# A three-layer graph network in one launch: the second norm moves to ScalarE, small columns to GpSimd, and VectorE's work is dealt out anew over the feed-forward slots

## The chip, the core and the metric

One core of a Trainium2 chip runs the whole program in one launch. The metric is the device time of that launch in microseconds (us). A core has TensorE (PE in the profile, its weight loads PEld), VectorE (DVE), ScalarE (ACT), GpSimd (POOL) and SyncE (SP, here only the queue of DMAs). Each engine takes its instructions in the order written and waits on semaphores for the others.

## The reference, cut to what matters

Input x is 8 graphs of 1024 nodes with 256 features. A first attention stage makes x; then come three layers, of which each does this:

```
si = x @ attn_w[l, :d];  sj = x @ attn_w[l, d:]
scores = si[:, :, None] + sj[:, None, :] + attn_b[l]
scores = where(scores >= 0, scores, 0.2 * scores);  scores = where(mask, scores, -inf)
attn = softmax(scores, axis=-1)
agg = einsum('bij,bjd->bid', attn, x)
h = layernorm(x + agg, g1[l], beta1[l])
ff = gelu(h @ W1[l] + b1[l]) @ W2[l] + b2[l]
x = layernorm(h + ff, g2[l], beta2[l])
```

At the very end the result is layernorm(x0 + x), x0 being what entered the three layers. Everything is in float32; to get that from TensorE each product is made of three (high by high, low by high, high by low part), so each operand is split into `_hi` (ScalarE) and `_lo` (VectorE).

## The kernel before

The change touches only `graph_layers`. The work is cut into K = 48 chunks of 512 nodes (3 layers of C = 16; two chunks make a graph). One **round** k works on three chunks at once: it aggregates chunk k (attention times x), runs the feed-forward of chunk k-1, and norms chunk k-2. Within a round TensorE first does `aggregate(k)` (8 source tiles j, 12 products each), then `up(k-1, 0)`, `up(k-1, 1)` and the residual, and then 8 **slots** f, in each `up(k-1, f+2)` and `down(k-1, f)`. Sixteen of the 48 rounds belong to each layer; rounds 2 to 33 norm a chunk whose projections the next layer needs, rounds 34 to 49 norm chunks of the last layer, which get the final norm instead.

What VectorE makes in round k, in its written order:

- `p_lo(k, 3..7)`: low parts of the probabilities, each 128x512. ScalarE's `exps(k, j)` go before them (two passes each), TensorE's `aggregate(k)` waits for them one by one. `p_lo(k, 0..2)` come at the end of round k-1.
- in between, `stats2(k-2)` and `centred(k-2)`: statistics of the second norm, and (Y - mean) * g2 from PSUM, 4 passes of 128x256.
- `row_top(r)`: the largest neighbour value of 128 rows (128x1024, one per row tile, four a round). Before: one ahead of `h_lo`, one at f = 3, one at f = 5, one at the end of the round.
- `h_lo(k-1)`, 2 passes, for which `up` waits; `scaled(k-2)`, 4 passes of xo * rstd + beta2; `projections(k-2)`, 8 passes (or `final_stats`).
- `norm1(k)`: reciprocal of the softmax sums, 4 passes u = A * rinv + x, 4 `bn_stats`, 4 `bn_aggr`.
- the slots: `g_lo(k-1, f)` (low part of the gelu, for which `down(k-1, f)` waits), `score(k+1, f)`, `add_mask(k+1, f-1)`; twice `x_lo`; once `shift1` (the norm's -mean * rstd); in even rounds after the first `g_lo` also `row_columns` (4 operations on 128x8) and `v_prepare` (4 more).

GpSimd only makes `deviation1` and `deviation2`: the variance plus eps, to the power -0.5, on 128x4. ScalarE's gelu of slot f needs `up(f)` and `g_lo(f-2)`. SP's queue loads the masks of `row_top` (three buffers), the transposed mask of chunk k+2 (its second half waits for the last `add_mask` of the round), and stores xo.

## Time and profile before

| | us |
|---|---|
| median of 3 runs | 2660.37 (2658.11 to 2666.33) |
| the profiled execution | 2659.89 |
| its span in the trace | 2657.7 |
| busy, of the span: PE, PEld, DVE, ACT, POOL | 2399.8 (90%), 2201.3 (83%), 2365.4 (89%), 1703.0 (64%), 517.7 (19%) |
| first and last start of `norm1` | 638.58 and 2589.78 |

Busy time is how long an engine had an instruction in work. Instructions of one engine overlap at their ends, so what one costs in a row of like ones is the distance of their starts (its pitch), a little less than its own duration. Where an instruction was kept waiting, the timeline shows in square brackets how long, and whose end released it. TensorE's clock is shown as a share of its full speed.

### The profile page before, as it was taken

The numbers are of one execution on the slowest core, as the hardware profiler recorded it, in microseconds if no ns is written. First come the engines' busy times: TensorE is split into PE (matmuls) and PEld (weight loads), VectorE is DVE, ScalarE is ACT, GpSimd is POOL, SyncE is SP. The second block draws the span as 40 slices with busy tenths as digits, with TensorE's granted clock in tenths as the row PEclk, the third lists the DMA queues.
The fourth block names the chain that finished last, engine by engine and source line by source line (L and its number), as shares of the span: only waits on it lengthen the run. The fifth ranks groups of instructions, "written<-read, shape, count | busy, mean of one in ns | idle before, by whom it ended". The sixth has DMA issues, their size and how long they took to land.

```text
span 2657.7 us, 45899 instructions
## 1 busy us (share of the span) xinstructions
PE 2399.8 (90%) x16548; PEld 2201.3 (83%) x16548; DVE 2365.4 (89%) x5742; ACT 1703.0 (64%) x2681; POOL 517.7 (19%) x500
## 2 busy tenths in 40 slices
PE   8999999963999999999889999999989999999996
PEld 6999999953888888888788888888878888888886
DVE  5888888878899999999889999999998999999985
ACT  3444444433676776777767776776776677677673
POOL 3555555530000001001010100100000110111111
PEclk9999999986999999999999999999999999999998
DMA  4444444444332322313232232332323234232211
GB/s 148 127 137 141 143 143 135 140 127 109 92 80 64 88 76 76 93 52 88 85 106 58 79 88 72 88 84 60 88 84 103 64 96 108 81 99 81 59 40 40
DMA packets 349875, 247.32 MB, mean 93 GB/s; under 512 B 214480, under 2 KB 308688, under 8 KB 349648
## 3 DMA queue, kind: packets, MB, share of 16 engines
q1 hardware_dynamic: 349648, 244.39, 32.1%
q8 instruction: 131, 2.15, 0.3%
q14 instruction: 96, 0.79, 0.1%
HBM read 143.68 MB, written 50.33 MB: 73 GB/s over the span
## 4 chain that ended last, share of the span: by engine, by line
PE 30%; DVE 23%; ACT 16%; issue 7%; DMA 2%; SPq 1%; ACTq 0%; POOLq 0%; DVEq 0%; POOL 0%
ACT t L964 6%; ACT pT_hi L963 5%; PE Y L1422 5%; PE G L45 4%; PE G L43 4%; PE G L44 4%; PE Y L1424 4%; PE Y L1423 4%; DVE prod L1177 3%; DVE u L1120 3%; DVE xo L1163 3%; DVE xo L1156 2%; ACT L963 2%; DVE spare L1072 2%; DVE st L1124 2%
## 5 line engine op out<-in xcount | busy, mean ns | idle before, releaser
L991 ACT ACTIVATE g<-G,b_less 128x512 f32<-128x512 f32 x384 | 264.0, 688 | 522.5 <-PE G L45 398.3
L1371 PE MATMUL A<-x_hi,pT_hi 128*128 128x258 f32 x1536 | 446.9, 291 | 114.8 <-DVE pT_lo L1108 114.8
L1422 PE MATMUL Y<-w_hi,g_hi 128*128 128x256 f32 x1536 | 441.1, 287 | 77.2 <-DVE g_lo L1206 77.2
L1372 PE MATMUL A<-x_hi,pT_lo 128*128 128x258 f32 x1536 | 437.8, 285 | 0.0
L1373 PE MATMUL A<-x_lo,pT_hi 128*128 128x256 f32 x1536 | 437.1, 285 | 0.0
L1424 PE MATMUL Y<-w_hi,g_lo 128*128 128x256 f32 x1536 | 429.8, 280 | 0.0
L1423 PE MATMUL Y<-w_lo,g_hi 128*128 128x256 f32 x1536 | 429.3, 279 | 0.0
L1371 PEld LDWEIGHTS A<-x_hi,pT_hi 128*128 128x128 f32 x1536 | 295.2, 192 | 125.3 <-issue 112.8
L1422 PEld LDWEIGHTS Y<-w_hi,g_hi 128*128 128x128 f32 x1536 | 289.4, 188 | 105.6 <-DVE g_lo L1206 97.3
L1206 DVE TENSOR_TENSOR g_lo<-g,g_hi 128x512 fp32r<-128x512 f32 x384 | 262.5, 684 | 67.3 <-ACT g_hi L994 65.3
L43 PE MATMUL G<-h_hi,w_hi 128*128 128x512 f32 x768 | 311.2, 405 | 5.7 <-DVE h_lo L1201 5.2
L45 PE MATMUL G<-h_lo,w_hi 128*128 128x512 f32 x768 | 306.7, 399 | 0.0
L44 PE MATMUL G<-h_hi,w_lo 128*128 128x512 f32 x768 | 305.8, 398 | 0.0
L1108 DVE TENSOR_TENSOR pT_lo<-t,pT_hi 128x512 fp32r<-128x512 f32 x384 | 254.7, 684 | 51.9 <-ACT t L964 51.1
L1423 PEld LDWEIGHTS Y<-w_lo,g_hi 128*128 128x128 f32 x1536 | 289.4, 188 | 8.2
L1372 PEld LDWEIGHTS A<-x_hi,pT_lo 128*128 128x128 f32 x1536 | 294.8, 192 | 0.0
L1373 PEld LDWEIGHTS A<-x_lo,pT_hi 128*128 128x128 f32 x1536 | 294.6, 192 | 0.0
L1424 PEld LDWEIGHTS Y<-w_hi,g_lo 128*128 128x128 f32 x1536 | 289.7, 189 | 0.0
L1096 DVE SCALAR_TENSOR_TENSOR t<-rrow,v 128x512 f32<-128x512 f32 x384 | 286.0, 745 | 2.6 <-ACT rrow L938 2.6
L917 POOL TENSOR_TENSOR ve<-mv,eps 128x4 f32<-128x4 f32 x64 | 30.0, 469 | 1320.8 <-DVE mv L1146 1178.9
L963 ACT ACTIVATE pT_hi<-t,v 128x512 fp32r<-128x512 f32 x384 | 272.9, 711 | 7.2 <-PE A L1373 6.7
L964 ACT ACTIVATE t<-t,v 128x512 f32<-128x512 f32 x384 | 272.1, 709 | 0.0
(176 smaller groups left out, 5857.0 us busy)
## 6 DMA issues: line engine op xcount, KB each, us to landing
mask<-mask SPq DMA_DIRECT2D x192, 256.0 KB, 3.3
a_adj_t<-in_adj SPq DMA_DIRECT2D x64, 512.0 KB, 4.0
x_rows<-rows SPq DMA_DIRECT2D x24, 1024.0 KB, 7.4
mask<-a_mask SPq DMA_DIRECT2D x64, 256.0 KB, 4.3
rows<-xo SPq DMA_DIRECT2D x32, 512.0 KB, 2.9
a_xs<-in_x SPq DMA_DIRECT2D x9, 1024.0 KB, 9.5
x_rows<-in_x SPq DMA_DIRECT2D x8, 1024.0 KB, 7.9
rows<-a_xo SPq DMA_DIRECT2D x64, 128.0 KB, 3.7
```

What stands on the lines that cost most here:

```text
L43: pe.matmul(out, left_hi, right_hi, start=start, stop=False)
L44: pe.matmul(out, left_lo, right_hi, start=False, stop=False)
L45: return pe.matmul(out, left_hi, right_lo, start=False, stop=stop)
L963: act.activation(L.pT[0][:, n % P_RING, :], L.t[:, j, :], ACT.Exp, bias=bias).then_inc(L.s_exp, 1)
L964: act.activation(L.t[:, j, :], L.t[:, j, :], ACT.Exp, bias=bias).then_inc(L.s_exp, 1)
L1096: dve.scalar_tensor_tensor(L.t[:, j, :], L.rrow[:, 0, k % 2, :], L.v8[:, k // 2 % VS, j:j + 1], L.rrow[:, 1, k % 2, :], ALU.add, ALU.max). ...
L1371: pe.matmul(L.A[:, t, 0:DE], hi, L.x_hi[:, par, j, :], start=(j == 0), stop=False)
L1372: pe.matmul(L.A[:, t, 0:DE], lo, L.x_hi[:, par, j, :], start=False, stop=False)
L1373: mm = pe.matmul(L.A[:, t, 0:D], hi, L.x_lo[:, par, j, :], start=False, stop=(j == NT - 1))
L1422: pe.matmul(L.Y[:, t, :], hi, L.w2[0][:, f, :], start=False, stop=False)
L1423: pe.matmul(L.Y[:, t, :], hi, L.w2[1][:, f, :], start=False, stop=False)
L1424: mm = pe.matmul(L.Y[:, t, :], lo, L.w2[0][:, f, :], start=False, stop=last and t % 2 == 1)
```

## The change

- `centred` on VectorE goes. ScalarE's new `n2(k-2)` writes (Y - mean) * rstd from PSUM into xo, four passes of 128x256, after `h(k-1, ...)`. `scaled` becomes two passes of 128x1024: times g2, then plus beta2. The wait for g2's load moves from `centred` to `scaled`.
- `row_columns` and `v_prepare` move from VectorE to GpSimd; there the columns are made in two halves of seven operations on 128x4, and -mean * rstd of both norms is made there too (two more operations each). `vrow`, `ub` and `top` become double.
- `norm1` is split: `sums` comes after `g_lo` of slot 0, `stats1` in slot 2. The eight passes of `projections` go two at a time into slots 1, 3, 5 and 7. In the last layer `final_sum` goes to slot 1, `final_stats` to 3, `final_norm` to 6.
- Three `row_top` stand ahead of the slots now (two ahead of `h_lo`, one behind), one in slot 5, none at the end.
- At the start, scoring begins after six row tops, and the seven of the next graph come after the low parts of chunk 0.

```diff
+    def rows_made(k):
+
+        return [n for n in ([2] if k == 0 else [(k + 5) // 2] if k % 2 == 1 else []) if n < NB]
...
-                    sp.wait_ge(L.s_scaled, TC * (m + 1))
+                    sp.wait_ge(L.s_scaled, 2 * (m + 1))
...
+            def row_columns(n, part):
+
+                done = COLS * n + COLS // NCH * part
+                cs = slice(TC * part, TC * (part + 1))
+                pool.wait_ge(L.s_top, NT * n + TC * (part + 1))
+                if part == 0:
+                    pool.wait_ge(L.s_vprep, 4 * (n + 1))
+                pool.tensor_tensor(L.z[:, cs], L.ub[:, n % 2, cs], L.top[:, n % 2, cs], ALU.add).then_inc(L.s_cols, 1)
+                pool.tensor_scalar(L.small[:, 1, cs], L.ub[:, n % 2, cs], SLOPE, None, ALU.mult).then_inc(L.s_cols, 1)
+                pool.wait_ge(L.s_cols, done + 2)
+                pool.tensor_scalar(L.small[:, 0, cs], L.z[:, cs], 0.0, 1.0 - SLOPE, ALU.is_ge, ALU.mult).then_inc(L.s_cols, 1)
+                pool.wait_ge(L.s_cols, done + 3)
+                pool.tensor_scalar(L.small[:, 0, cs], L.small[:, 0, cs], SLOPE, None, ALU.add).then_inc(L.s_cols, 1)
+                pool.wait_ge(L.s_cols, done + 4)
+                pool.tensor_tensor(L.m[:, cs], L.small[:, 0, cs], L.z[:, cs], ALU.mult).then_inc(L.s_cols, 1)
+                pool.wait_ge(L.s_cols, done + 5)
+                if n >= 1:
+                    pool.wait_ge(L.s_rrowT, NCH * n)
+                pool.tensor_tensor(L.rcol[:, 0, cs], L.ub[:, n % 2, cs], L.m[:, cs], ALU.subtract).then_inc(L.s_cols, 1)
+                pool.tensor_tensor(L.rcol[:, 1, cs], L.small[:, 1, cs], L.m[:, cs], ALU.subtract).then_inc(L.s_cols, 1)
...
+                if k >= 1:
+                    pool.wait_ge(L.s_n1, TC * k)
...
+                pool.wait_ge(L.s_rs, 4 * k + 1)
                 pool.tensor_tensor(L.rstd[:, :], L.ve[:, :], L.half[:, :], ALU.pow).then_inc(L.s_rs, 1)
...
+                pool.tensor_tensor(L.nm[:, :], L.mv[:, :, 0], L.minus[:, :], ALU.mult).then_inc(L.s_rs, 1)
+                pool.wait_ge(L.s_rs, 4 * k + 3)
+                pool.tensor_tensor(L.nmr[:, :], L.nm[:, :], L.rstd[:, :], ALU.mult).then_inc(L.s_rs, 1)
+
+            def deviation2(m):
+                if m >= 1:
+                    pool.wait_ge(L.s_n2, TC * m)
+                pool.wait_ge(L.s_mv2, TC * (m + 1))
+                pool.tensor_tensor(L.ve2[:, :], L.mv2[:, :, 1], L.eps[:, :], ALU.add).then_inc(L.s_rs2, 1)
+                pool.wait_ge(L.s_rs2, 4 * m + 1)
+                pool.tensor_tensor(L.rstd2[:, :], L.ve2[:, :], L.half[:, :], ALU.pow).then_inc(L.s_rs2, 1)
+                pool.tensor_tensor(L.nm2[:, :], L.mv2[:, :, 0], L.minus[:, :], ALU.mult).then_inc(L.s_rs2, 1)
+                pool.wait_ge(L.s_rs2, 4 * m + 3)
+                pool.tensor_tensor(L.nmr2[:, :], L.nm2[:, :], L.rstd2[:, :], ALU.mult).then_inc(L.s_rs2, 1)
...
+            v_prepare(0)
+            for part in range(NCH):
+                row_columns(0, part)
+            v_prepare(1)
             for k in range(K + 2):
                 if k >= 2:
-                    deviation2(L.s_mv2, TC * (k - 1), L.s_rs2, k - 2)
-                i = k - 2 - (K - C)
-                if i >= 0:
-                    deviation2(L.s_fin_mv, TC * (i + 1), L.s_fin_rs, i)
+                    deviation2(k - 2)
+                if k % 2 == 0 and (k + 2) // 2 < NB:
+                    for part in range(NCH):
+                        row_columns((k + 2) // 2, part)
+                for n in rows_made(k):
+                    v_prepare(n)
                 if k < K:
                     deviation1(k)
+                if k - 2 >= K - C:
+                    deviation3(k - 2 - (K - C))
...
-                if n >= 1:
-                    act.wait_ge(L.s_top, NT * n)
-                act.activation(L.vrow[:, :].rearrange("p (c i) -> p c i", c=2), L.A[:, 2:4, :], ACT.Copy).then_inc(L.s_vrow, 1)
+                if n >= 2:
+                    act.wait_ge(L.s_top, NT * (n - 1))
+                act.activation(L.vrow[:, n % 2, :].rearrange("p (c i) -> p c i", c=2), L.A[:, 2:4, :], ACT.Copy).then_inc(L.s_vrow, 1)
...
-                    act.wait_ge(L.s_nmr, k + 1)
+                    act.wait_ge(L.s_rs, 4 * (k + 1))
                 act.activation(L.u[:, t, :], L.u[:, t, :], ACT.Identity, bias=L.nmr[:, t:t + 1],
                                scale=L.rstd[:, t:t + 1]).then_inc(L.s_n1, 1)
+
+            def n2(m):
+                act.wait_ge(L.s_rs2, 4 * (m + 1))
+                if m >= 1:
+                    act.wait_ge(L.s_xst, 16 * m)
+                for t in range(TC):
+                    act.activation(L.xo[:, t, :], L.Y[:, t, :], ACT.Identity, bias=L.nmr2[:, t:t + 1],
+                                   scale=L.rstd2[:, t:t + 1]).then_inc(L.s_n2, 1)
...
+                if k >= 2:
+                    n2(k - 2)
...
+                    if f == 3:
+                        for n in rows_made(k):
+                            copy_v(n)
...
-            def norm1(k):
+            def sums(k):
...
+
+            def stats1(k):
+                n = TC * k
...
-            def shift1(k):
-
-                dve.wait_ge(L.s_rs, 2 * (k + 1))
-                if k >= 1:
-                    dve.wait_ge(L.s_n1, TC * k)
-                dve.scalar_tensor_tensor(L.nmr[:, :], L.mv[:, :, 0], -1.0, L.rstd[:, :], ALU.mult, ALU.mult).then_inc(L.s_nmr, 1)
 
...
-            def centred(m):
-
-                if m >= 1:
-                    dve.wait_ge(L.s_xst, 16 * m)
+            def scaled(m):
+                dve.wait_ge(L.s_n2, TC * (m + 1))
                 if new_layer(m):
                     dve.wait_ge(L.s_g2_in, 32 * (layer_of(m) + 1))
-                dve.wait_ge(L.s_mv2, TC * (m + 1))
-                for t in range(TC):
-                    dve.scalar_tensor_tensor(L.xo[:, t, :], L.Y[:, t, :], L.mv2[:, t, 0:1], L.g2[:, :], ALU.subtract,
-                                             ALU.mult).then_inc(L.s_n2, 1)
-
-            def scaled(m):
-                dve.wait_ge(L.s_rs2, 2 * (m + 1))
-                for t in range(TC):
-                    dve.wait_ge(L.s_n2, TC * m + t + 1)
-                    dve.scalar_tensor_tensor(L.xo[:, t, :], L.xo[:, t, :], L.rstd2[:, t:t + 1], L.be2[:, :], ALU.mult,
-                                             ALU.add).then_inc(L.s_scaled, 1)
-
-            def projections(m):
+                dve.tensor_tensor(L.xo[:, :, :], L.xo[:, :, :], L.g2[:, :].unsqueeze(1).to_broadcast([P, TC, D]),
+                                  ALU.mult).then_inc(L.s_scaled, 1)
+                dve.wait_ge(L.s_scaled, 2 * m + 1)
+                dve.tensor_tensor(L.xo[:, :, :], L.xo[:, :, :], L.be2[:, :].unsqueeze(1).to_broadcast([P, TC, D]),
+                                  ALU.add).then_inc(L.s_scaled, 1)
+
+            def projections(m, tiles):
 
                 slot = m % C
-                dve.wait_ge(L.s_scaled, TC * (m + 1))
-                if new_layer(m):
-                    dve.wait_ge(L.s_aw_in, 32 * (layer_of(m) + 1))
-                for t in range(TC):
+                if 0 in tiles:
+                    dve.wait_ge(L.s_scaled, 2 * (m + 1))
+                    if new_layer(m):
+                        dve.wait_ge(L.s_aw_in, 32 * (layer_of(m) + 1))
+                for t in tiles:
                     for i in range(2):
...
+            def final_sum(m):
...
+                dve.wait_ge(L.s_scaled, 2 * (m + 1))
+                dve.tensor_tensor(L.xo[:, :, :], L.xo[:, :, :], L.x1[:, :, :], ALU.add).then_inc(L.s_fin, 1)
+
...
-            v_prepare(0)
-            for r in range(NT):
+            for r in range(NT - 2):
                 row_top(r)
-            row_columns(0)
-            v_prepare(1)
             for j in range(NT):
                 score(0, j)
                 add_mask(0, j)
+                if j == HALF - 1:
+                    for r in range(NT - 2, NT):
+                        row_top(r)
...
-            for r in range(NT, NT + NT - 1):
-                row_top(r)
...
                 tops = tops_of(k)
+                early = 3 if k >= 1 else 1
                 if agg:
                     p_lo(k, LEAD)
                 if old:
                     stats2(k - 2)
                 if agg:
-                    for j in range(LEAD + 1, NT - 1):
+                    for j in range(LEAD + 1, NT):
                         p_lo(k, j)
-                if old:
-                    centred(k - 2)
-                if agg:
-                    p_lo(k, NT - 1)
-                for r in tops[:1]:
+                if k == 0:
+                    for r in range(NT, NT + NT - 1):
+                        row_top(r)
+                for r in tops[:min(early, 2)]:
                     row_top(r)
                 if ffn:
                     h_lo(k - 1)
+                for r in tops[2:early]:
+                    row_top(r)
                 if old:
                     scaled(k - 2)
-                if projected:
-                    projections(k - 2)
-                elif old:
-                    final_stats(k - 2)
                 if ffn and new_layer(k - 1):
                     less_b2(layer_of(k - 1))
-                if agg:
-                    norm1(k)
                 for f in range(KF):
                     if ffn:
                         g_lo(k - 1, f)
-                    if f == 0 and k % 2 == 0:
-                        if (k + 2) // 2 < NB:
-                            row_columns((k + 2) // 2)
-                        if (k + 4) // 2 < NB:
-                            v_prepare((k + 4) // 2)
+                    if f == 0 and agg:
+                        sums(k)
+                    if f == 2 and agg:
+                        stats1(k)
+                    if f in (1, 3, 5, 7) and projected:
+                        projections(k - 2, (f // 2,))
                     if after:
                         score(k + 1, f)
                         if f >= 1:
                             add_mask(k + 1, f - 1)
-                    if f == 1 and old and not projected:
-                        final_norm(k - 2)
-                    if f == 2 and agg:
-                        shift1(k)
+                    if old and not projected:
+                        if f == 1:
+                            final_sum(k - 2)
+                        if f == 3:
+                            final_stats(k - 2)
+                        if f == 6:
+                            final_norm(k - 2)
                     if f in (4, 6) and k + 2 < K:
                         x_lo(k + 2, f // 2 - 2)
-                    if f in (3, 5):
-                        for r in tops[f // 2:f // 2 + 1]:
+                    if f == 5:
+                        for r in tops[early:]:
                             row_top(r)
                     if f >= 4 and agg and new_layer(k):
                         weights_lo(layer_of(k), f - 4)
@@ -1313,8 +1361,6 @@
                     add_mask(k + 1, KF - 1)
                 if agg and new_layer(k):
                     weights_lo(layer_of(k), KF - 4)
-                for r in tops[3:]:
-                    row_top(r)
                 if after:
                     for j in range(LEAD):
...
-                pe.wait_ge(L.s_cols, 4 * (k // 2 + 1))
+                pe.wait_ge(L.s_cols, COLS // NCH * (k + 1))
...
-                pe.wait_ge(L.s_vrow, min((k + 5) // 2, NB))
+                pe.wait_ge(L.s_vrow, 2 if k == 0 else min(k // 2 + 3, NB))
...
-                        if k % 2 == 0 and k + 4 < K:
-                            v_row((k + 4) // 2)
+                        for n in rows_made(k):
+                            v_row(n)
```

## Rows read from the trace of the kernel before

**Rows 1.** Windows: one round; busy us of each engine, PEclk, DMA share, GB/s.
```profile
1556.12:1597.13 41.01, 37.86 (x273) 35.04 (x272) 39.10 (x99) 30.06 (x47) 3.48 (x4) 1.00 0.24 65
```

**Rows 2.** Timeline, TensorE, one round: start, us, instruction, idle before and its releaser.
```profile
1581.97 0.36 PE L1371 MATMUL A<-x_hi,pT_hi 128*128 128x258 f32 x1 [1.55 <-DVE pT_lo L1108]
...
1594.42 0.39 PE L43 MATMUL G<-h_hi,w_hi 128*128 128x512 f32 x1
...
1601.23 0.38 PE L1422 MATMUL Y<-w_hi,g_hi 128*128 128x256 f32 x1 [1.57 <-DVE g_lo L1206]
```

**Rows 3.** Timeline, VectorE, the same round.
```profile
1581.14 1.29 DVE L1108 TENSOR_TENSOR pT_lo<-t,pT_hi 128x512 fp32r<-128x512 f32 x2
...
1594.36 0.42 DVE L1177 SCALAR_TENSOR_TENSOR prod<-xo,aw 128x256 f32<-128x256 f32 x1
...
1597.13 0.17 DVE L1113 RECIPROCAL rinv<-A 128x4 f32<-128x4 f32 x1
...
1598.92 1.40 DVE L1124 BATCH_NORM_STATS2 st<-u 128x6 f32<-128x256 f32 x4
...
1600.51 0.66 DVE L1206 TENSOR_TENSOR g_lo<-g,g_hi 128x512 fp32r<-128x512 f32 x1
...
1602.35 0.74 DVE L1096 SCALAR_TENSOR_TENSOR t<-rrow,v 128x512 f32<-128x512 f32 x1
...
1603.02 0.68 DVE L1102 TENSOR_TENSOR t<-t,maskT 128x512 f32<-128x512 f32 x1
...
1603.62 0.68 DVE L1206 TENSOR_TENSOR g_lo<-g,g_hi 128x512 fp32r<-128x512 f32 x1
...
1613.96 1.22 DVE L1072 CUSTOM_DVE_ANT_0 spare<-vrow,mask 128x1024 bf16<-128x1024 f32 x1
...
1615.11 0.68 DVE L1206 TENSOR_TENSOR g_lo<-g,g_hi 128x512 fp32r<-128x512 f32 x1
...
1621.34 1.29 DVE L1108 TENSOR_TENSOR pT_lo<-t,pT_hi 128x512 fp32r<-128x512 f32 x2
```

**Rows 4.** Timeline, ScalarE, the same round.
```profile
1588.01 0.71 ACT L964 ACTIVATE t<-t,v 128x512 f32<-128x512 f32 x1
...
1590.61 0.77 ACT L974 ACTIVATE h_hi<-G,shift,g 128x512 fp32r<-128x512 f32 x1
...
1596.60 0.68 ACT L994 ACTIVATE g_hi<-G,b_less 128x512 fp32r<-128x512 f32 x1
```

**Rows 5.** Timeline, VectorE: starts of the first operation of `norm1` in six rounds.
```profile
724.36 0.17 DVE L1113 RECIPROCAL rinv<-A 128x4 f32<-128x4 f32 x1
...
1292.88 0.18 DVE L1113 RECIPROCAL rinv<-A 128x4 f32<-128x4 f32 x1
...
1346.22 0.17 DVE L1113 RECIPROCAL rinv<-A 128x4 f32<-128x4 f32 x1
...
1434.70 0.18 DVE L1113 RECIPROCAL rinv<-A 128x4 f32<-128x4 f32 x1
...
2103.74 0.15 DVE L1113 RECIPROCAL rinv<-A 128x4 f32<-128x4 f32 x1
...
2470.01 0.15 DVE L1113 RECIPROCAL rinv<-A 128x4 f32<-128x4 f32 x1
```

**Rows 6.** Timeline, VectorE, a round of the last layer.
```profile
2263.85 1.23 DVE L1214 TENSOR_TENSOR xo<-xo,x 128x1024 f32<-128x1024 f32 x1
...
2273.17 1.38 DVE L1226 TENSOR_SCALAR xo<-xo,mv,rstd 128x256 f32<-128x256 f32 x4
```

**Rows 7.** Timeline, GpSimd: first an otherwise idle stretch, then the round above.
```profile
642.21 0.20 POOL L911 TENSOR_TENSOR ve<-mv,eps 128x4 f32<-128x4 f32 x1 [59.34 <-DVE mv L1129]
...
1600.67 0.55 POOL L911 TENSOR_TENSOR ve<-mv,eps 128x4 f32<-128x4 f32 x1 [12.47 <-DVE mv L1129]
...
1601.31 2.00 POOL L913 TENSOR_TENSOR rstd<-ve,half 128x4 f32<-128x4 f32 x1
```

**Rows 8.** Timeline, VectorE, two rounds after the first change of layer.
```profile
1381.97 1.66 DVE L1156 SCALAR_TENSOR_TENSOR xo<-Y,mv,g 128x256 f32<-128x256 f32 x4 [3.14 <-DMA be<-in_L_gnn_beta]
```

More of the change, by code:

```diff
@@ L672, in layer_buffers @@
     L.v2 = sb("v2", [P, VS, NT])
-    L.top = sb("top", [P, NT])
+    L.top = sb("top", [P, 2, NT])
     L.z = sb("z", [P, NT])
+    L.small = sb("small", [P, 2, NT])
     L.m = sb("m", [P, NT])
     L.rcol = sb("rcol", [P, 2, NT])
-    L.vrow = sb("vrow", [P, N])
+    L.vrow = sb("vrow", [P, 2, N])
     L.rrow = sb("rrow", [P, 2, 2, BANK])
@@ L775, in graph_layers @@
     HALF = NT // 2
+    COLS = 7 * NCH
     EARLY = 5
@@ L1005, in _ @@
             x_hi(0)
+            for part in range(2):
+                copy_rows(0, part)
             x_hi(1)
-            for k in range(2):
-                for part in range(2):
-                    copy_rows(k, part)
+            exps(0, 0)
+            for part in range(2):
+                copy_rows(1, part)
+            exps(0, 1)
             copy_v(1)
-            for j in range(LEAD):
-                exps(0, j)
-            for k in range(K + 1):
-                ffn = k >= 1
+            exps(0, 2)
+            for k in range(K + 2):
+                ffn = 1 <= k <= K
                 for j in range(LEAD, NT):
```

88 lines of the change are left out of this document (40 added, 48 removed).

## The prediction

> **What bounds the kernel now.** I read the windows first. In a full round TensorE is busy 37.86 of 41.01 us, VectorE 39.10, ScalarE 30.06, GpSimd 3.48, and TensorE's clock is granted in full [rows 1]. VectorE has the least air, but a busy share says nothing about which of its work is on the path. So next I looked at where TensorE stands still, in its own timeline. There are two gaps a round: 1.55 us ahead of `aggregate`, ended by `p_lo`, and 1.57 us ahead of `down(0)`, ended by `g_lo` [rows 2]. Everything else of TensorE is packed. Its own work thus needs 41.01 - 1.55 - 1.57 = 37.9 us, and both gaps are VectorE's doing.
>
> VectorE's and ScalarE's timelines show why [rows 3, 4]. I count from the start of `p_lo(k, 0)` at 1581.14. Aggregation starts at +0.83, `up(0)` at +13.28 [rows 2], and ScalarE's second gelu pass of slot 0 ends at 1597.28, so +16.14 [rows 4]. `g_lo(0)` could start there. It starts at 1600.51, +19.37: VectorE is first held by projections (1594.36 to 1597.13), sums (to 1598.92) and statistics (to 1600.51) [rows 3]. From `g_lo(0)` to the next `p_lo(0)` it then has 1621.34 - 1600.51 = 20.83 us of slots [rows 3]. So the round is one loop: `p_lo(0)`, all that VectorE does before `g_lo(0)`, the slots, `p_lo(0)`. Over 14 rounds of the first layer it takes (1292.88 - 724.36) / 14 = 40.61 us, even and odd together [rows 5].
>
> **What the change makes of that loop.** After it, the stretch before `g_lo(0)` holds less for VectorE and the slots hold more. Two questions decide: does VectorE still reach `g_lo(0)` last, and how long are the slots?
>
> *Up to `g_lo(0)`.* The last exponential ends at 1588.72, +7.58 [rows 4], so `p_lo(7)` ends by +8.2 (pitch of a 128x512 pass with two inputs: 1603.62 - 1603.02 = 0.60 [rows 3]). Two row tops at 1615.11 - 1613.96 = 1.15 each [rows 3] bring +10.5, `h_lo` (2 x 0.60) +11.7, which is ahead of `up(0)` at +13.28; the third top +12.9. `scaled` is now two wide passes. The trace has one such pass, the last layer's sum, at 1.23 us [rows 6]; with the wait of the second for the first I take 2.5. It needs `n2`. ScalarE is done with `h` at 1591.38, +10.24 [rows 4]. No row shows a 256-column pass from PSUM on it; the nearest is the 512-column `h` at 0.77 [rows 4]. Half of that is the lower bound, the whole the upper: 4 passes are 1.5 to 3.1 us. I take 2.2, since a pass has a fixed part. `n2` then ends at +12.4, at worst +13.3, and `scaled` at +15.4, at worst +15.8. ScalarE has no gelu to make until `up(0)` is through, so `n2` is hidden in its wait. All of this is before +16.14. So TensorE's aggregation and ScalarE's gelu now end last, and `g_lo(0)` starts at about +16.2. What is taken off VectorE here (`centred`, half the fixed cost of `scaled`) buys nothing beyond that point: the rest becomes VectorE's idle time, 0.4 to 0.8 us or more.
>
> *The slots.* By pitches [rows 3]: eight `g_lo` 4.80; eight scores at 1603.02 - 1602.35 = 0.67, 5.36; eight `add_mask` 4.80; two `x_lo` 1.20; sums 1598.92 - 1597.13 = 1.79; statistics 1600.51 - 1598.92 = 1.59; projections 1597.13 - 1594.36 = 2.77; one row top 1.15. Together 23.46 us, where 20.83 stood: 6.15 come in; two tops, `shift1` and some waits on ScalarE go out. The columns (`row_columns`, `v_prepare`) leave VectorE here too, in even rounds, so even and odd rounds become alike.
>
> The new loop is 16.2 + 23.4 = **39.6 us**, above TensorE's 37.9, so VectorE's slots and the aggregation share the path and TensorE's two gaps become one, ahead of `aggregate`, with a short one at `down(7)`. Gain 1.0 us a round. TensorE is not late anywhere else: `down(1)` to `down(6)` follow their `g_lo` by one to three us.
>
> *The last layer* differs. No projections (2.77) but 1.23 + 1.59 + 1.38 = 4.2 us of final sum, statistics and norm [rows 3, 6], and these now all fall in the slots: 16.2 + 23.4 - 2.8 + 4.2 = 41.0. Before, it was (2470.01 - 2103.74) / 9 = 40.70 [rows 5]. These rounds lose 0.3 each.
>
> *Changes of layer.* Between 1292.88 and 1346.22 one round takes 53.34 us because weights arrive two pieces at a time [rows 5]; that chain goes through VectorE's and ScalarE's slots in the same way and I leave it. The two rounds after it take 88.48 [rows 5], 44.2 each. In the second of them `centred` waits 3.14 us for beta2 to land [rows 8]; the wait now belongs to `scaled`, some 6 us later in the round, where the load is there or nearly. So I take 2 x 39.6 here: 9.3 gained, and 8 at the second change, where one of the two is already a last-layer round.
>
> *GpSimd.* It gets 14 small operations in an even round, 4 in an odd one, and two more for each norm. One takes 0.20 us in a quiet stretch and 0.55 in the round; the power takes up to 2.00 [rows 7]. Deviation 2, whose statistics stand between the low parts, is made before the row tops; 14 columns at 0.65 with their waits take 9 us from the first row top at +9.4, so until +18.5; TensorE reads them in slot 2, past +21. Deviation 1: the statistics end at +24.0, then 0.55 + 2.00 + 0.55 + 0.55 and gaps, ready at +28. `n1` stands behind gelu(5), which ends at about +29. All hidden; without that cover the columns would cost their 9 us. What waits behind `n1` on ScalarE is gelu(6), and VectorE asks for that only at about +34.
>
> *Loads.* SP issues the masks after the round's last `add_mask`. That moment now lies right at `p_lo(0)` and the first row top stands earlier, so their lead shrinks by some 2 us. The store waits for `scaled`, a little later than before, and `n2` of the next round for the store, most of a round later: nothing.
>
> *Head and tail.* At the head seven row tops (8 us) move behind the first low parts, and scores start after six tops and a GpSimd chain. At most 8 us, at least 0; I take 5 with the first two rounds, since these tops still stand before the first `sums`. At the tail nothing hides the chain: two more GpSimd operations, `n2` in place of `centred` that ran beside GpSimd, a wider `scaled`: +3.
>
> **Sum.** 27 rounds x 1.0 = -27; changes of layer -17; nine last-layer rounds +3; head -5; tail +3: -43. Against the profiled execution's 2659.9 (its span plus 2.2 around it, within 0.5 of the median 2660.4) that gives **2616 us**.
>
> **A rule against the change.** GpSimd's variance sum takes 0.55 in place of 0.20 us while VectorE is working, and VectorE's `g_lo` beside it starts its successors on the usual pitch [rows 3, 7]. So the trace has GpSimd paying and VectorE not. The Trainium skill says more (SBUF — State Buffer, section "Who interferes with whom"): a VectorE instruction with two SBUF inputs and a GpSimd instruction that reads SBUF exclude each other for a whole instruction, and who starts first decides. Nearly all of VectorE's slot work is of that kind. The trace agrees with the one half; the other half, VectorE held, no row here shows. As a mechanism of this kernel it is the third rival below.
>
> **The rivals.**
> 1. *The changes of layer keep their time* (weights, loads of g2, and TensorE's clock after long gaps): only the 27 rounds gain. -26 with the other terms, 2634. For it: I argued these 17 us from a wait of 3.14 and a loop, not from a walk through them.
> 2. *VectorE isn't held at +16.2 or the slots overlap better*, and TensorE's 37.9 is approached. At 38.5 a round: -30 more, 2585. Against it: the slots' pitches are measured, and no idle time is in them.
> 3. *Slower: GpSimd holds VectorE.* If each of the four operations of deviation 1 and the 18 of the columns and preparation stop a VectorE instruction for their free 0.20 (the power for about 1.0), slots and run-up lose 1.6 and some 2 us: the loop passes 41.6. From 1.0 us lost a round the gain is gone; at 2 it is +27 in the 27 rounds and +20 in the last layer, less the changes of layer: about 2685. Against it: the two operations per norm that are there today cost VectorE nothing visible.
> 4. *No change:* a new wait takes about 1 us a round (masks that land late ahead of the three row tops, `n1` held by GpSimd by over 4 us, or `scaled` held so that `g_lo(0)` is at +17.2): 2655.
>
> **Chances.** The forecast 0.60 (own range 2604 to 2628), rival 1 0.15, rival 2 0.05, rival 3 0.10, rival 4 0.10. A measurement here can tell about 0.3%, 8 us. Faster takes the forecast, rivals 1 and 2 and a little of 4: 0.82; same 0.07; slower 0.11. The range reaches from a loop of 39.2 with the head at its bound, 2600, to rival 1 with a loop 0.3 worse, 2643.
>
> **What would show it.** Starts of the reciprocal 39.6 us apart, equal in even and odd rounds, and 41.0 in the last layer; VectorE idle for a microsecond or so ahead of `g_lo(0)`, released by ScalarE's gelu; TensorE's gap ahead of `down(0)` gone and the one ahead of `aggregate` over 2 us; no wait on GpSimd in ScalarE's list. It is wrong if `g_lo(0)` still stands behind VectorE's own work, if VectorE's 128x512 passes show a pitch above 0.60 beside GpSimd's, or if row tops wait for masks.

## The result and the profile after

The changed kernel takes 2622.18 us (median of 4 runs, 2618.43 to 2623.29) against 2659.89 for the kernel before: a ratio of 0.9848, with 0.9833 to 0.9862 as its interval. The forecast was 2616, range 2600 to 2643. The profiled execution took 2618.43 us, its span 2616.6.

First the windows of two successive rounds of the kernel after, cut at the starts of the reciprocal (columns: length, busy time and count of each engine, granted clock, DMA share, GB/s):

```profile
1529.73:1569.26 39.53, 37.01 (x266) 34.35 (x265) 37.04 (x85) 30.96 (x50) 8.63 (x12) 1.00 0.31 75
1569.26:1608.77 39.51, 37.54 (x274) 35.02 (x273) 37.30 (x84) 31.89 (x51) 14.67 (x22) 1.00 0.30 86
```

Against [rows 1], VectorE's busy time has fallen by 2 us and GpSimd's has risen from 3.48 to 8.63 and 14.67. Both rounds last 39.5 us, as forecast (39.6).

VectorE's timeline of the same kernel, one run-up to `g_lo(0)`:

```profile
1552.53 2.49 DVE L1166 TENSOR_TENSOR pT_lo<-t,pT_hi 128x512 fp32r<-128x512 f32 x4
...
1558.69 0.69 DVE L1166 TENSOR_TENSOR pT_lo<-t,pT_hi 128x512 fp32r<-128x512 f32 x1 [0.28 <-ACT t L1041]
1559.31 1.22 DVE L1143 CUSTOM_DVE_ANT_0 spare<-vrow,mask 128x1024 bf16<-128x1024 f32 x1
...
1561.83 1.28 DVE L1248 TENSOR_TENSOR h_lo<-h,h_hi 128x512 fp32r<-128x512 f32 x2
...
1564.18 1.22 DVE L1206 TENSOR_TENSOR xo<-xo,g 128x1024 f32<-128x1024 f32 x1
1565.43 1.22 DVE L1209 TENSOR_TENSOR xo<-xo,be 128x1024 f32<-128x1024 f32 x1
1568.65 0.69 DVE L1253 TENSOR_TENSOR g_lo<-g,g_hi 128x512 fp32r<-128x512 f32 x1 [2.00 <-ACT g_hi L1079]
1569.26 0.17 DVE L1171 RECIPROCAL rinv<-A 128x4 f32<-128x4 f32 x1
```

and ScalarE's and TensorE's of that stretch:

```profile
1561.22 1.92 ACT L1065 ACTIVATE xo<-Y,nmr,rstd 128x256 f32<-128x256 f32 x4
...
1567.35 0.69 ACT L1076 ACTIVATE g<-G,b_less 128x512 f32<-128x512 f32 x1 [2.91 <-PE G L45]
1567.93 0.68 ACT L1079 ACTIVATE g_hi<-G,b_less 128x512 fp32r<-128x512 f32 x1
```

```profile
1553.36 0.36 PE L1417 MATMUL A<-x_hi,pT_hi 128*128 128x258 f32 x1 [1.60 <-DVE pT_lo L1166]
...
1565.76 0.40 PE L43 MATMUL G<-h_hi,w_hi 128*128 128x512 f32 x1
...
1570.78 0.28 PE L1468 MATMUL Y<-w_hi,g_hi 128*128 128x256 f32 x1
```

Counted from `p_lo(0)` at 1552.53, aggregation starts at +0.83, `up(0)` at +13.23, `n2` ends at +10.6, and the second wide pass of `scaled` ends at +14.1. VectorE then stands still for 2.00 us until ScalarE's gelu lets `g_lo(0)` go at +16.12. In every other round the last low parts wait 1.0 us for ScalarE's exponentials first, and 0.99 us is left ahead of `g_lo(0)`; the start is at +16.12 all the same:

```profile
1529.12 0.69 DVE L1253 TENSOR_TENSOR g_lo<-g,g_hi 128x512 fp32r<-128x512 f32 x1 [0.99 <-ACT g_hi L1079]
```

Before, there was no such wait and `g_lo(0)` stood at +19.37 [rows 3]. TensorE has no gap ahead of `down(0)` any more (1570.78 has no bracket); the one ahead of `aggregate` is 1.60, as before [rows 2].

GpSimd's timeline, and then its lines by group for 1569 to 2000 us (busy us, mean ns of one, idle before):

```profile
1576.69 2.08 POOL L966 TENSOR_TENSOR ve<-mv,eps 128x4 f32<-128x4 f32 x1 [14.08 <-DVE mv L1190]
1578.85 1.10 POOL L968 TENSOR_TENSOR rstd<-ve,half 128x4 f32<-128x4 f32 x1
```

```profile
L966 POOL TENSOR_TENSOR ve<-mv,eps 128x4 f32<-128x4 f32 x11 | 22.9, 2086 | 119.2 <-DVE mv L1190 119.2
...
L977 POOL TENSOR_TENSOR ve<-mv,eps 128x4 f32<-128x4 f32 x10 | 10.9, 1091 | 167.1 <-DVE mv L1200 167.1
...
L948 POOL TENSOR_TENSOR z<-ub,top 128x4 f32<-128x4 f32 x10 | 5.2, 522 | 0.0
...
L953 POOL TENSOR_SCALAR small<-small 128x4 f32<-128x4 f32 x10 | 10.0, 1004 | 0.8
```

Of its small operations one costs 0.2 to 2.1 us in this stretch, where [rows 7] had 0.20 and 0.55 for the variance sum. It is hidden all the same, as the chain of waits for 900 to 2600 us shows (us in total, times, longest):

```profile
DVE g_lo L1253 <- ACT g_hi L1079: 95.5, 56, 5.0
...
DVE xo L1206 <- ACT xo L1065: 7.8, 7, 2.3
ACT xo L1065 <- POOL nmr L982: 7.4, 9, 1.7
...
DVE spare L1143 <- DMA mask<-mask: 3.4, 6, 0.9
...
ACT u L1057 <- POOL nmr L971: 0.9, 1, 0.9
```

Where did the 41.1 us of span go? The starts of `g_lo(0)` in both timelines cut the span into stretches that mean the same in both kernels:

| stretch | before | after | difference | forecast |
|---|---|---|---|---|
| start to `g_lo(0)` of round 2 | 727.73 | 722.11 | -5.6 | -5 |
| rounds 2 to 16, 14 of them | 568.53 | 553.39 | -15.1 | -14 |
| three rounds at the first change of layer | 141.82 | 135.09 | -6.7 | -9.3 |
| 13 rounds of the second layer | 527.53 | 513.76 | -13.8 | -13 |
| three rounds at the second change | 141.48 | 137.80 | -3.7 | -8 |
| nine rounds of the last layer | 366.27 | 367.22 | +1.0 | +3 |
| last three rounds | 119.78 | 121.00 | +1.2 | 0 |
| from there to the end | 64.56 | 66.23 | +1.7 | +3 |

The first row can't be counted for the change. In a second trace of the same changed kernel this stretch took 727.36 us, and in the traces of the kernels below 721.70 to 728.37. Of the 5.6 us, 3.6 lie ahead of the first row top (587.66 before, 584.11 after). The full rounds, in contrast, agree within 0.2 us over 14 and over 13 of them in the changed kernel's two traces.

### The profile page after: what moved, and what is told of

Its sections match the earlier page's. It is cut to its first block, busy times and chain, and to the rows that moved or that the text cites. A ratio compares the mean times of both kernels' runs of the same rounds, so it can differ in the third digit from the quotient of the medians.

```text
span 2616.6 us, 46231 instructions
## 1 busy us (share of the span) xinstructions
PE 2385.6 (91%) x16548; PEld 2200.0 (84%) x16548; DVE 2293.9 (88%) x5214; ACT 1793.4 (69%) x2873; POOL 986.1 (38%) x1125
## 4 chain that ended last, share of the span: by engine, by line
DVE 24%; PE 18%; issue 6%; ACT 2%; DMA 0%; POOL 0%; POOLq 0%; SPq 0%; DVEq 0%; ACTq 0%
DVE t L1154 5%; PE A L1417 5%; DVE t L1160 5%; PE A L1418 4%; PE A L1419 4%; DVE g_lo L1253 4%; DVE prod L1224 2%; DVE x_lo L1232 1%; DVE st L1185 1%; DVE spare L1143 1%; DVE u L1178 1%; PE G L1399 1%; PE G L45 1%; ACT g_hi L1079 1%; PE G L43 1%
## 5 line engine op out<-in xcount | busy, mean ns | idle before, releaser
L977 POOL TENSOR_TENSOR ve<-mv,eps 128x4 f32<-128x4 f32 x48 | 53.6, 1117 | 711.7 <-DVE mv L1200 711.7
L966 POOL TENSOR_TENSOR ve<-mv,eps 128x4 f32<-128x4 f32 x48 | 91.2, 1901 | 528.9 <-DVE mv L1190 528.9
L1166 DVE TENSOR_TENSOR pT_lo<-t,pT_hi 128x512 fp32r<-128x512 f32 x384 | 247.4, 691 | 37.4 <-ACT t L1041 37.2
```

## Experiments

All kernels start from the changed one. Ratios are to the kernel before, measured on the same chip; it took 2658.9 to 2660.8 us there. The changed kernel, measured a second time (beside the kernels of 4, 8 and 9), took 2621.12, 0.9846 (0.9824 to 0.9868).

**1. The second norm back on VectorE.** `centred` comes back between `p_lo(6)` and `p_lo(7)`, `scaled` is four passes again, `n2` is gone:

```diff
-                if k >= 2:
-                    n2(k - 2)
...
+                if old:
+                    centred(k - 2)
+                if agg:
+                    p_lo(k, NT - 1)
```

> Edit: the second norm goes back to VectorE (four passes of Y - mean times g2 ahead of the last p_lo, then four narrow passes with rstd and beta2), all else as in the changed kernel. My theory (a round is one loop: from p_lo(0) over TensorE's aggregation and ScalarE's gelu to g_lo(0), then VectorE's slots): VectorE gets 1.57 us more and 0.9 us less ahead of g_lo(0), where it idles 1.6 to 2.0 us, so the loop stays at 39.5 us and the time within 5 us of the changed kernel's 2622; the tail gets some 3 us shorter, and at a change of layer the fold waits less. Rival (VectorE's busy time sets the round): 0.7 us more in each of 46 rounds, 2652.

Measured: 2627.13 us, 0.9878 (0.9862 to 0.9895). The 13 rounds of a layer are 39.5 us each, as with `n2`. So in the rounds the new norm is worth nothing; its work was in the wait ahead of `g_lo(0)`. In all it is worth 5 us by the medians, and by the ratios (0.9878 against 0.9848 and 0.9846) 8 us, hardly more than the intervals allow. The traces show gains and losses. The round after the weights round is 43.46 and 44.35 us without `n2`, where it was 39.54 and 39.53, and the waits name the reason, the one of [rows 8]:

```profile
DVE xo L1204 <- DMA be<-in_L_gnn_beta: 10.9, 2, 5.9
```

The weights rounds themselves are shorter without `n2` (54.52 and 55.14 us), and so is the tail (63.97 against 66.2).

**2. and 3. The columns back on VectorE, in two places.** `row_columns` and `v_prepare` as before the change, once behind `g_lo(0)`, once ahead of it, in the wait:

```diff
+                columns(k)
```

ahead of the loop over the slots, or in it:

```diff
                     if ffn:
                         g_lo(k - 1, f)
+                    if f == 0:
+                        columns(k)
```

> Edit: row_columns and v_prepare go back to VectorE, behind g_lo of slot 0 (one of them in each round, about 0.7 us of small operations), all else as in the changed kernel. My theory: they lengthen the slots one for one, loop 40.2 us, and with 46 rounds about +30 us: 2650. Rival (GpSimd's many small operations hold VectorE): taking them off GpSimd gives part of it back, loop 39.5 to 39.8, 2622 to 2635. A GpSimd operation will also be shorter.

> Edit: as the kernel with the columns on VectorE in slot 0, but placed behind scaled, ahead of g_lo(0), where VectorE idles 1.6 to 2.0 us. My theory: the same operations are free here, loop 39.5 us, time 2622 within 5 us. Rival (VectorE's busy time sets the round, or GpSimd holds it): the same time as the kernel with them in slot 0.

Measured: in the slot 2641.07 us, 0.9933 (0.9917 to 0.9949), rounds of 39.9 and 40.1; ahead of `g_lo(0)` 2619.13, 0.9845 (0.9827 to 0.9864), rounds of 39.52. The same operations cost some 20 us behind `g_lo(0)`, and nothing that can be told from the noise ahead of it, one pass of 0.6 us earlier. The slots grow by 0.35 us in one round (`v_prepare`) and 0.57 in the next (`row_columns`), 0.46 on average, and the round by as much: one for one, as the first expectation has it, which had taken the operations at 0.7 us and so came to 2650. A timeline of the second kernel shows why: with them VectorE still waits.

```profile
1571.17 0.22 DVE L1096 TENSOR_SCALAR ub<-uv,ab 128x8 f32<-128x8 f32 x1
...
1573.13 0.69 DVE L1242 TENSOR_TENSOR g_lo<-g,g_hi 128x512 fp32r<-128x512 f32 x1 [1.59 <-ACT g_hi L1027]
```

So moving the columns to GpSimd was not needed for this gain. Once the order leaves a wait ahead of `g_lo(0)`, they fit there.

**4. Twelve more operations on GpSimd a round**, on 128x4 data of their own:

```diff
+                    for i in range(12):
+                        if 12 * k + i:
+                            pool.wait_ge(L.s_extra, 12 * k + i)
+                        pool.tensor_tensor(L.extra[:, i, :], L.eps[:, :], L.minus[:, :], ALU.mult).then_inc(L.s_extra, 1)
                     deviation1(k)
```

> Edit: twelve more operations of 128x4 with two inputs on GpSimd in each round, ahead of the first norm's deviation; they compute nothing that is used. My theory: hidden, GpSimd has 25 us of idle time a round; loop 39.5 us, time as the changed kernel within 3 us, VectorE's pitches as they are (0.60 for 128x512). Rival 3 of the prediction (GpSimd's reads hold VectorE): each costs VectorE up to 0.20 us, 2.4 us a round, partly in its idle time: loop 40.5 or more, 2665.

Measured: 2622.39 us, 0.9856 (0.9833 to 0.9879); rounds of 39.53. A window of one round:

```profile
1537.58:1577.10 39.52, 36.99 (x267) 34.32 (x266) 37.07 (x84) 30.96 (x50) 20.20 (x32) 1.00 0.34 76
```

GpSimd is now busy half the round (before the change: 3.48 of 41 us), and VectorE's busy time is still 37.07. Its 128x512 passes with two inputs keep their pitch of 0.60, and its slots stay at 23.41 us. Rival 3, GpSimd stopping VectorE by enough to be seen in a round, is refuted.

**5. The order back, the rest kept.** Projections, sums and statistics ahead of `g_lo(0)` again, row tops in their old places:

```diff
-                early = 3 if k >= 1 else 1
+                early = 1
...
+                if projected:
+                    projections(k - 2, range(TC))
+                if agg:
+                    sums(k)
+                    stats1(k)
                 for f in range(KF):
```

> Edit: VectorE's old order (projections, sums and statistics ahead of g_lo(0); row tops in slots 3 and 5 and at the end; final norm's parts as before), with the second norm on ScalarE and the columns on GpSimd kept. My theory: g_lo(0) is again held by VectorE's own work, at about +19.2, and the slots are 19.5 us plus about 1 us of waits on ScalarE: loop 39.8 us, even and odd alike, time about 2635. So most of the gain would come from the columns leaving the slots and from what is shed ahead of g_lo(0), and 0.3 us a round from the dealing. Rival (the dealing is what gains): loop 40.4 or more, 2655.

Measured: 2751.66 us, 1.0358 (1.0324 to 1.0392). This expectation failed: 2635 was expected, 2655 by its rival, and the rounds alternate at 41.4 and 43.9. The new norm and the columns on GpSimd, without the dealing out, make the kernel 3.6% slower than it was. Its rows, VectorE, TensorE and windows:

```profile
1545.55 1.23 DVE L1206 TENSOR_TENSOR xo<-xo,g 128x1024 f32<-128x1024 f32 x1 [1.12 <-ACT xo L1065]
...
1554.23 0.67 DVE L1253 TENSOR_TENSOR g_lo<-g,g_hi 128x512 fp32r<-128x512 f32 x1
```

```profile
1554.94 0.39 PE L1467 MATMUL Y<-w_hi,g_hi 128*128 128x256 f32 x1 [3.08 <-DVE g_lo L1253]
...
1556.42 0.59 PE L43 MATMUL G<-h_hi,w_hi 128*128 128x512 f32 x1
1556.81 0.63 PE L44 MATMUL G<-h_hi,w_lo 128*128 128x512 f32 x1
```

```profile
1515.00:1519.00 4.00, 4.00 (x26) 3.56 (x25) 3.98 (x7) 2.05 (x3) 2.84 (x3) 1.00 0.00 0
...
1556.40:1560.40 4.00, 4.00 (x18) 3.34 (x16) 2.88 (x5) 2.02 (x3) 2.86 (x3) 0.57 0.01 2
```

Two things were not in my sum. `scaled`, which in the old order is reached early, waits 1.12 us for `n2`, so `g_lo(0)` stands at +20.76 instead of +19.37. And TensorE's gap ahead of `down(0)` has grown to 3.08 us; behind it, in every second round, 4 us pass at a granted clock of 0.57 (mostly the lower of its two levels, 1.2 GHz), and a product over 512 columns takes 0.63 us instead of 0.39. In the other rounds the gap is as long (3.10 at 1513.52) and the clock stays at 1.00. Two more kernels took these apart.

**6. The same, with `up(2)` computed twice** into the same bank. It gives TensorE six more products in that gap and changes no result:

```diff
-                for i in range(KD):
+                for i in [i for _ in range(2 if f == 2 else 1) for i in range(KD)]:
```

> The order of before with the new norm and the columns on GpSimd (as in the kernel that took 2751.7 us), and one addition: the up product of the third feed-forward slot, up(2), is computed twice into the same bank, so that TensorE has 1.4 us less of idle time ahead of down(0). In that kernel's trace the gap ahead of down(0) was 3.08 us in each round, and in every second round (43.9 us, against 41.4) the granted clock stood at 0.57 from 1.5 us behind the gap on, for 4 us, and matmuls of 128x512 took 0.63 us instead of 0.39. Theory A (the long gap lowers the granted clock, and that costs the 2.5 us): with the gap at 1.7 us, as long as the one that the kernel before has there, the clock stays at 1.00, all rounds are 41.4 us, and 20 rounds win 2.5: about 2700 us. Theory B (the rounds of 43.9 us are those in which vcol's rows are transposed, and that work costs the 2.5 us by itself): the distances stay 41.4 and 43.9, about 2752 us. Theory C (TensorE's own work is what sets the pace of this order): the six extra matmuls, 1.4 us, are added in 47 rounds, up to 2815 us.

Measured: 2720.73 us, 1.023 (1.0213 to 1.0247). The gap ahead of `down(0)` and a window at the place where the clock was down:

```profile
1537.87 0.39 PE L1467 MATMUL Y<-w_hi,g_hi 128*128 128x256 f32 x1 [1.66 <-DVE g_lo L1253]
```

```profile
1541.00:1545.00 4.00, 4.00 (x32) 3.70 (x31) 3.91 (x6) 2.55 (x4) 1.19 (x1) 1.00 0.01 2
```

More work on TensorE makes the kernel 31 us faster: the gap is 1.66, the clock stays full, the long rounds fall from 43.9 to 42.3. Theory A holds for 1.6 of the 2.5 us. The last 0.9 is left; it stands in the rounds in which the `vcol` rows are transposed and copied, where theory B has it.

**7. The order back and the norm back** (the edits of 1 and 5 together). Of the change the columns on GpSimd, the first norm's `nmr` there and the new start stay.

> The order of before and the norm of before (both norm passes on VectorE); of the change only the small columns on GpSimd stay, with their double buffers. Theory A (the order with the new norm lost by its 1.1 us wait of scaled for ScalarE's n2 and by the clock behind the long gap; the columns on GpSimd cost nothing in either order): g_lo(0) comes at +19.4 us behind p_lo(0) as in the kernel before, the gap ahead of down(0) is 1.6 us, the clock stays up, and the columns' 0.8 us is out of every second round: 40.2 us in all, 2660 - 0.8 x 23 = about 2642 us (2635 to 2650). Theory B (the columns or the first norm's small operations on GpSimd come late in the old order): rounds of 41 us or more, 2690 to 2750 us. In both the rounds at the two changes of layer keep the times of the kernel before, 53 and 44 us.

Measured: 2651.64 us, 0.9970 (0.9957 to 0.9983). VectorE's `g_lo(0)` and the next `p_lo(0)`, two rounds:

```profile
1636.59 0.66 DVE L1257 TENSOR_TENSOR g_lo<-g,g_hi 128x512 fp32r<-128x512 f32 x1
...
1657.26 1.29 DVE L1161 TENSOR_TENSOR pT_lo<-t,pT_hi 128x512 fp32r<-128x512 f32 x2
...
1676.64 0.66 DVE L1257 TENSOR_TENSOR g_lo<-g,g_hi 128x512 fp32r<-128x512 f32 x1
...
1698.16 1.28 DVE L1161 TENSOR_TENSOR pT_lo<-t,pT_hi 128x512 fp32r<-128x512 f32 x2
```

The slots are 20.67 and 21.52 us, before the change 20.83 [rows 3] and 21.64. The time lies above theory A's 2635 to 2650: with the columns gone from VectorE, even and odd rounds still differ, by 0.9 us (40.03 and 40.92). VectorE waits for the gelu twice in the long round, 1.66 us in all, where the short round has one wait of 0.88:

```profile
1685.33 0.69 DVE L1257 TENSOR_TENSOR g_lo<-g,g_hi 128x512 fp32r<-128x512 f32 x1 [0.53 <-ACT g_hi L1076]
...
1689.02 0.69 DVE L1257 TENSOR_TENSOR g_lo<-g,g_hi 128x512 fp32r<-128x512 f32 x1 [1.13 <-ACT g_hi L1076]
```

Before the change the long round had the columns (0.9 us by experiment 2) and waits of 0.66 and 0.13 us. So two branches of nearly the same length lie behind that difference, and taking the columns off VectorE alone uncovers the other: it wins 0.1 to 0.2 us a round.

Read as a path, the kernels give each part a price. Columns on GpSimd and the new start take 2660 to 2651.64 us; the dealing out, with the old norm, takes it to 2627.13 (experiment 1), some 24 us and the only large step; the norm on ScalarE takes it to 2622. Against experiment 5 the old norm is 100 us faster in the old order: 1.39 us in each of 46 rounds (`g_lo(0)` back from +20.76 to +19.37) and the 1.6 us of the clock in every second one make 101. In the new order it is 5 to 8 us slower.

**8. and 9. More work into the wait.** VectorE stands still ahead of `g_lo(0)` for 2.00 and 0.99 us in turn. If 1.6 to 2.0 us there are free, as I took it, a fourth row top (1.2 us), or that and one projection, should go there for nothing and make the slots shorter:

```diff
-                early = 3 if k >= 1 else 1
+                early = 4 if k >= 1 else 1
...
+                if projected:
+                    projections(k - 2, (0,))
```

(the last two lines in the second kernel alone, which leaves that projection out of slot 1)

> Edit: the fourth row top too stands ahead of the slots (behind h_lo) in place of slot 5. My theory: the slots lose 1.15 us, the stretch ahead of g_lo(0) has 1.6 to 2.0 us of air: loop 38.4 us, in the last layer 39.6, time about 2573. What could spoil it: its mask has only three buffers and is loaded only after the first row top of the round, so it may wait some tenths of a us. Rival (VectorE's busy time sets the round): no change, 2622.

> Edit: as the kernel with four row tops ahead of the slots, and the first pair of projections too ahead of g_lo(0), in place of slot 1. My theory: the slots lose 0.7 us more (in rounds that project), the air ahead of g_lo(0) is used up; TensorE's own work, 37.0 us in odd rounds and 37.9 in those with the extra transposes, and the chain from the last gelu over the first exponentials come close: loop 37.8 to 38.2 us in the first two layers, 39.6 in the last, time about 2560.

Measured: 2613.73 us, 0.9822 (0.9802 to 0.9842), rounds alternating at 38.38 and 39.80; 2615.72, 0.9833 (0.9812 to 0.9854), rounds of 38.8 and 39.5. Both expectations failed: of 49 us expected the first kernel gives 8, and the projections add nothing to it. A round of the first two layers gives 0.4 of the 1.15 us, and the last layer nothing (40.9 us on average, 39.6 expected): the row tops' masks, which the expectation named, are waited for there for 6.7 us in all, 2.6 at most (2050 to 2500 us). VectorE's timeline of the first kernel, in a long round:

```profile
1508.33 1.40 DVE L1166 TENSOR_TENSOR pT_lo<-t,pT_hi 128x512 fp32r<-128x512 f32 x2
1510.26 0.69 DVE L1166 TENSOR_TENSOR pT_lo<-t,pT_hi 128x512 fp32r<-128x512 f32 x1 [0.54 <-ACT t L1041]
1511.49 0.69 DVE L1166 TENSOR_TENSOR pT_lo<-t,pT_hi 128x512 fp32r<-128x512 f32 x1 [0.53 <-ACT t L1041]
...
1516.40 0.73 DVE L1166 TENSOR_TENSOR pT_lo<-t,pT_hi 128x512 fp32r<-128x512 f32 x1 [0.53 <-ACT t L1041]
...
1525.76 0.69 DVE L1253 TENSOR_TENSOR g_lo<-g,g_hi 128x512 fp32r<-128x512 f32 x1
```

The shorter slots bring VectorE to `p_lo(0..4)` before ScalarE's exponentials are done: three waits of 0.53 to 0.54 and one of 0.19. It then reaches `g_lo(0)` at +17.4 with its own work, without a wait, instead of at +16.1. VectorE's run-up had become the longer branch. It had least room in this parity before: the changed kernel has the 0.99 us wait there. ScalarE makes the exponentials without a gap behind the last gelu, and that one waits for TensorE's `up(7)`; shorter slots of VectorE don't bring it forward by as much.

**10. Two projections ahead instead.**

```diff
+                if projected:
+                    projections(k - 2, (0, 1))
...
-                    if f in (1, 3, 5, 7) and projected:
+                    if f in (5, 7) and projected:
```

> The changed kernel with two of the four projections of a round (1.4 us of VectorE's work) ahead of g_lo(0), where VectorE waits 2.0 us for the gelu, instead of in slots 1 and 3; the third row top stays where it is. Theory A (the loop is p_lo(0), aggregation, up(0), gelu, and then VectorE's slots alone): each round is 1.4 us shorter, 38.1, and the time 2622 - 1.4 x 31 = 2578 us. Theory B (what one more row top ahead showed: half of the rounds are then paced by ScalarE's exps, which the shorter slots reach before they are done, so that VectorE comes to g_lo(0) late): distances alternate at 38.4 and 39.5 or so, about 2600 to 2616 us. Theory C (the masks' transfers held the kernel with one more row top): no wait here for masks, and the time falls under 2590.

Measured: 2605.04 us, 0.9791 (0.9776 to 0.9805), rounds mostly of 39.2 and 38.9. Theory B: 0.5 us a round is won of 1.4. Again `g_lo(0)` starts without a wait, at 1558.20 or +17.1, and in 18 of some 28 rounds `n1` waits for GpSimd (29.2 us in all, 900 to 2000 us), as here:

```profile
1548.80 0.71 DVE L1166 TENSOR_TENSOR pT_lo<-t,pT_hi 128x512 fp32r<-128x512 f32 x1 [0.53 <-ACT t L1041]
...
1558.20 0.69 DVE L1253 TENSOR_TENSOR g_lo<-g,g_hi 128x512 fp32r<-128x512 f32 x1
```

```profile
1533.15 1.10 ACT L1057 ACTIVATE u<-u,nmr,rstd 128x256 f32<-128x256 f32 x2 [2.14 <-POOL nmr L971]
```

That wait isn't what the gain is lost to. Where a pair of rounds has none, the distances are 38.21 and 39.84, and where it has waits of 2.14 and 0.82 us they are 39.20 and 38.92: 78.1 us for the pair either way, against 79.05 in the changed kernel.

**11. The same, and in the last layer `final_sum` ahead of `g_lo(0)`.**

```diff
+                elif old:
+                    final_sum(k - 2)
```

> The kernel with two projections ahead of g_lo(0) (2605.0 us), and in the last layer, which has no projections, the final sum (one pass of 1.23 us) ahead of g_lo(0) as well instead of in slot 1. In the changed kernel's last layer VectorE waits 1.9 us ahead of g_lo(0) for the gelu, so theory A (what stands ahead of g_lo(0) within that wait is free) says that each of the some 10 full last-layer rounds goes from 40.8 to 39.6 us, at the two or three last rounds nothing: 2605 - 12 = about 2593 us. Theory B (half of it goes to waits for ScalarE's exps and n2, as when work was moved there in the other layers, 0.45 of 1.4 us won a round): about 2600 us. Theory C (the last layer is held by its loads of x1 or by the masks): no change or worse, 2605 us or above.

Measured: 2598.53 us, 0.9775 (0.9759 to 0.9792). Most rounds of the last layer are 39.6 to 39.8 us instead of 40.76, as by theory A, a few still 40.4 to 40.5. In the traces the last-layer rounds win 13.2 us, and the two profiled executions are 13.0 us apart (2592.00 and 2605.03). The medians are only 6.5 us apart, and the intervals of the two ratios overlap, so which theory has the size right stays open. This is the fastest kernel of the case: 0.9775 of the kernel before, where the changed one stands at 0.9846 to 0.9848.

## Why the prediction was right, point by point

**The loop.** `p_lo(0)`, aggregation, `up(0)`, gelu, `g_lo(0)`, slots: forecast 16.2 + 23.4 = 39.6, measured 16.12 + 23.4 = 39.52, even and odd. That VectorE's work up to `g_lo(0)` no longer counts is shown by experiments 1 and 3, that each microsecond added to the slots counts by experiment 2. Taking work out of the slots does not give the same back (experiments 8 to 10). `n2` took 1.92 where I took 2.2, `scaled` 2.5 as taken. Four signs that I named came differently. TensorE's gap ahead of `aggregate` did not grow past 2 us; it is 1.60, and the rest of the idle time went to small ones behind `g_lo` (0.79 ahead of `down(7)`). VectorE's idle time ahead of `g_lo(0)` is 2.0 and 0.99 us in turn, not about 1. ScalarE's list does have waits on GpSimd (`n2` 7.4 us in nine, `n1` 0.9 in one), and row tops do wait for masks (3.4 us in six, all in the last layer), which I had called a sign of being wrong; neither is large enough to matter. Two slips of the working changed nothing: its terms add up to 2617, not 2616, and the slots before did have idle time in them (0.87 us ahead of one `g_lo`, for the gelu), which rival 2 denies.

**The reason for equal rounds was half of it,** though the number was right. I put the 0.8 us between even and odd rounds down to VectorE's columns alone; experiment 7 has the difference without them. In all four kernels of the old order it is in the rounds with the `vcol` transposes (1.04 us on TensorE) and the copy of `vrow` (1.03 us on ScalarE); which of the two does it was not tried. With the slots as full as after the change it disappears: VectorE has no wait in the slots of these rounds.

**Changes of layer: the term was too large,** -17 forecast, -10.4 measured. The two rounds behind each weights round gained 9.4 (88.48 to 79.07; forecast 9.3) and 6.8 (87.05 to 80.29; forecast 8). The step that failed is the one I did not walk: "that chain goes through VectorE's and ScalarE's slots in the same way and I leave it". The weights round itself went from 53.34 to 56.02 and from 54.43 to 57.51. In it the projections, sums and statistics now stand in front of the `w_lo` passes, the fold of b2 waits for `n2`, and `g_lo(0)` for the gelu. TensorE, VectorE and the clock there, in the kernel after:

```profile
1322.23 0.35 PE L1443 MATMUL Y<-b_parts,w_hi 128*128 128x2 f32 x2 [0.56 <-ACT xo L1065]
```

```profile
1331.52 0.69 DVE L1253 TENSOR_TENSOR g_lo<-g,g_hi 128x512 fp32r<-128x512 f32 x1 [5.03 <-ACT g_hi L1079]
```

```profile
1326.00:1332.00 6.00, 5.64 (x23) 4.45 (x23) 0.82 (x3) 3.06 (x5) 0.00 (x0) 0.75 0.25 87
```

The clock is down to 0.75 in those 6 us, and it was before, too (0.72 in the matching 6 us). These rounds also vary from one execution to the next: 57.84 and 54.93 us in the changed kernel's second trace. Experiment 1 points at `n2`: without it they take 54.52 and 55.14 us, where 18 such rounds in the nine traces with `n2` in the new order take 53.9 to 57.8, 56.3 on average. With one trace of that kernel this is a hint and no proof; how the 2.7 and 3.1 us are divided was not separated.

**Last layer, head, tail.** Last layer 40.8 instead of 41.0, so +1 and not +3 for nine rounds: its wait for the gelu is 1.4 to 2.3 us, its slots are 0.3 shorter than summed. Head -5.6 for -5 is luck: that stretch was 727.36 in the second trace, -0.4. Tail +1.7 for +3, and the last three rounds +1.2 that I had at nothing.

**GpSimd.** Hidden, as said, but not at the price said: the variance sum of the first norm was taken at 0.55 and takes 2.09. It stayed hidden because the statistics end at +24.1, as summed, the power takes 1.10 us where 2.00 was taken, so that the chain ends at +28.5 (forecast +28), and `n1` stands behind gelu(5), 1.2 us later; the list has one wait of 0.9 us for it. Experiment 10 shows how thin this is: with slots 1.4 us shorter `n1` waits up to 2.14.

**The rivals.** Rival 1 (changes of layer keep their time) was true for two fifths of its 17 us. Rival 2 (38.5 a round) did not come; even with VectorE's wait filled, in experiments 10 and 11, the rounds stay at 39.05 on average. Rival 3 is refuted by experiment 4: GpSimd's operations grow longer beside VectorE, VectorE's do not. The Trainium skill (SBUF — State Buffer, section "Who interferes with whom") lets the first to start block the other; VectorE's slot passes follow each other without a gap, and the `ve` sum at 1576.69 lasts over three of them (score at 1576.46, the mask's pass at 1577.09, `g_lo` at 1577.70, the next pass 0.60 us later, all at their usual distances). That would fit the rule with GpSimd as the one that loses each time; that the lock is what lengthens its operations, and that VectorE's passes start first because they are back to back, is inferred. Rival 4: its waits are there (`scaled` for `n2` 7.8 us, masks 3.4, `n1` 0.9), but over 43 rounds none makes 0.2 us a round.

## What to carry to other kernels

When a loop has two branches that meet at one instruction, price each edit by the branch it is in: the same column operations on VectorE cost 0 or 20 us, 0.6 us apart. Work moved ahead of the meeting point is free only until that branch ends last, and it ends later than the idle time suggests, because the producers don't come earlier by as much as the rest was shortened (here over half of the gain in a round went to waits for ScalarE's exponentials). Look at the idle time in both kinds of round; the smaller one counts as well. A change of several parts can't be priced as their sum: the norm on ScalarE was worth 5 to 8 us in the new order and minus 100 in the old one.

## What the runs showed of the hardware

- A TensorE gap of 3.1 us ahead of `down(0)` went with a granted clock of 0.57 over the 4 us that began 1.5 us after it, in every second round; the same gap in the other rounds did not. With 1.4 us of repeated products in the gap the clock stayed at 1.00, and the kernel got 31 us faster.
- GpSimd's variance sum on 128x4 takes 0.55 us in the rounds before and 2.09 in the rounds after; means by line of its small operations go from 0.52 (L948) over 1.00 (L953) to 2.09 (L966). While VectorE stood still (from 1528.13 to 1529.12 us of the kernel after) they took 0.20. VectorE's own pitch did not change, with GpSimd busy 3.5 or 20 us a round. The 0.20 us of [rows 7] fell beside VectorE's passes on 128x8, not beside an idle VectorE.
